# A fused attention and adapter-network block: logits, values and fills in pairs of steps, gate rows later, half an output projection earlier

## The chip, the cores and the metric

The kernel runs on one core of one Trainium2 chip. The metric is the device time of one launch in microseconds (us). The kernel before took 1315.23 us as the median of three runs, from 1310.58 to 1323.12.

## The reference

Everything is float32: a batch of 2 sequences of 2048 tokens with 256 features.

```python
mod = (silu(c) @ wmod).reshape(2, 6, 1, -1)          # sa, ca, ga, sb, cb, gb
ga, gb = bounded away from zero, at least 0.25 in size
h = layernorm(x) * (1 + ca) + sa
q, k, v = split(h @ W_qkv.T + b_qkv)                 # 16 heads of 16 features
o = softmax(causal(q k^T / 4)) v
x = x + ga * (o @ W_out.T + b_out)
h = layernorm(x) * (1 + cb) + sb
mole(x, W, b, A, B, R) = x W + b + 1/8 * sum_e softmax(x R)_e * (x A_e) B_e   # 3 experts, rank 8
return x + gb * mole(relu(mole(h, W1, ...)), W2, ...)    # 256 -> 1024 -> 256
```

## The kernel before, in words

The 4096 tokens are eight blocks of 512. To keep float32's precision, an operand of most products is split into a high part (rounded) and a low part (the rest), and a product is three passes, high x high, high x low, low x high (`product`, L391). The split's high part is mostly written by ScalarE (ACT), the low part by VectorE (DVE).

**First stage.** For each block DVE normalises x, TensorE (PE) transposes it (`turn`, L761), ACT scales and shifts it (`modulate`, L1024), DVE makes the low part (L1153), PE projects to queries and keys (`project_qk`, four chunks of six matmuls over 512 columns) and to values (`project_v`, 24 matmuls over 256 columns); ACT and DVE write high and low parts of queries and keys (L1031, L1165), which SyncE's queue (SP) stores to HBM and loads back as stacks of heads (L438, L453). Ahead of block 0's projections PE computes the modulation columns (L742) and the sixteen matmuls of the two gate rows (`gate_rows`, L751), which ACT copies out (L1046) before it goes on to block 1. GpSimd (POOL) clears rows of the stacks meanwhile (L585).

**Attention** runs over 32 units (4 heads of one sequence and 512 queries), in 320 steps of 128 keys. The logits stand transposed (keys on partitions), and the row maximum has to be known before a step: it is taken in advance from a second computation of the logits with queries on partitions. So PE has three kinds of work. `logits` (L875): four matmuls a step, one a head, on 64 rows of the array each, two heads at a time on the two halves, into three banks in turn. ACT takes the exponential of each (L1074) into `prob`. `values` (L893): eight matmuls of a step (four heads beside one another on 32 columns each, in two float32 passes), accumulated in one bank; they run two steps behind (`PV_LAG`). `fill` (L855): a tile of the maximum computation for a later unit, mostly four or two matmuls, that DVE reduces (L1222, L1218) out of two double banks. Diagonal tiles and steps get a mask added by small bf16 matmuls (L811). PE's order in a step: `values(n-2)`, logits of heads 0 and 1, up to two fills, logits of heads 2 and 3, more fills. Which fills stand in which step is a table (`ORDER`, made by `slots`); it holds 610 fills and isn't changed. A logit matmul waits until the exponential three before it is done (its bank), a fill until DVE has reduced the tile two before it.

**The network.** For each block i PE computes eight inner tiles (`hidden`, six matmuls over 512 columns and one low-rank matmul L954) in two banks; ACT empties each twice with relu (L1114: full, then high part) and DVE subtracts to the low part (`hid_low`, L1365). In between stand the low-rank tail of block i-1 and, after the fourth tile, the output projection of block i+1 (`project_out`, 24 matmuls). DVE then makes its residual, statistics and normalised rows, PE transposes them, and so on; `down` (L965) is the second layer, four groups of 24 matmuls, whose first one follows the high and low parts as they come. The projection's operand `oT` is split by ACT (`o_high`, L1084) and DVE (`low_o`, L1260) at the head of block i, after POOL has normalised the loaded rows (L694). POOL also adds residuals (L710, L699). Each engine works in the order written; waits are on semaphores.

## Time and profile before

| | |
|---|---|
| median of three runs | 1315.23 us |
| the profiled execution's own time | 1316.99 us |
| its span | 1315.0 us |
| PE busy | 1222.3 us (93%), 9456 matmuls |
| DVE busy | 934.4 us (71%) |
| ACT busy | 800.2 us (61%) |
| POOL busy | 183.3 us (14%) |
| mean clock granted to PE | 0.959 of full speed |

The profile is of one execution. Its times count from the span's start. A matmul's duration reaches from its start to a modelled end, and the next may stream earlier; what separates two of them is read from their starts. The idle time in brackets is that of the engine just before the instruction, with what ended it.

### The profile page before, as it was taken

To read this page: it belongs to the slowest core of one execution; us is meant where nothing else is said; L and a number is where in the kernel's file an instruction comes from. 1 tells how busy PE (TensorE), PEld (TensorE's weight loads), DVE (VectorE), ACT (ScalarE), POOL (GpSimd) and SP (SyncE) were. 2 spreads that over 40 slices of the span, in tenths; PEclk is the share of its full clock that TensorE was granted. 3 is DMA by queue.
4 is the path that set the end of the run, shared out by engine and by line. 5 is a ranking of instruction groups with operands and counts; after the bars stand their busy time and mean duration, and the time that the engine had idled before them with its cause. 6 is when DMAs were issued, how large, how long until landed. Compare 5 with 4: busy or idle time off the path is not lost.

```text
span 1315.0 us, 23664 instructions
## 1 busy us (share of the span) xinstructions
PE 1222.3 (93%) x9456; PEld 709.5 (54%) x9456; DVE 934.4 (71%) x1247; ACT 800.2 (61%) x1611; POOL 183.3 (14%) x153
## 2 busy tenths in 40 slices
PE   7988789999999999999999999999989999999997
PEld 6765333444444344444444444334334888888886
DVE  4877897888787888777888778776531477776653
ACT  4441466777667777767777767776664455454442
POOL 5205600000112000000000000201010133232310
PEclk9997799999999999999999989999787999999998
DMA  5793120031142022022022013400000122211100
GB/s 169 245 289 140 51 64 10 16 83 29 35 107 60 9 64 54 10 62 71 10 54 56 10 32 102 113 1 9 11 10 22 45 64 65 54 50 38 53 17 33
DMA packets 58118, 79.53 MB, mean 60 GB/s; under 512 B 12680, under 2 KB 28752, under 8 KB 58008
## 3 DMA queue, kind: packets, MB, share of 16 engines
q1 hardware_dynamic: 58008, 78.01, 20.3%
q8 instruction: 75, 1.23, 0.4%
q14 instruction: 35, 0.29, 0.1%
HBM read 47.57 MB, written 29.62 MB: 59 GB/s over the span
## 4 chain that ended last, share of the span: by engine, by line
PE 68%; DVE 17%; ACT 8%; issue 4%; SPq 2%; DMA 2%; ACTq 0%; DVEq 0%
PE ps L893 21%; PE ps L875 17%; PE ps L855 9%; PE ps L965 7%; PE ps L391 6%; ACT prob L1074 6%; PE ps L811 6%; DVE mx L1222 5%; DVE hid_lo L1365 4%; DVE xhat L419 1%; DVE stats L409 1%; SPq L453 1%; DMA xs<-in_x 1%; ACT o_sb L1059 1%; DVE x L1270 1%
## 5 line engine op out<-in xcount | busy, mean ns | idle before, releaser
L1074 ACT ACTIVATE prob<-ps 128x512 f32<-128x512 f32 (+3 forms) x1280 | 597.8, 536 | 267.9 <-PE ps L811 137.9
L1222 DVE TENSOR_REDUCE mx<-ps 128x2 f32<-128x1024 f32 (+1 forms) x512 | 591.5, 1187 | 164.1 <-PE ps L855 92.9
L875 PE MATMUL ps<-qst,kst 64*128 64x512 f32 (+3 forms) x1280 | 379.5, 450 | 14.9 <-ACT prob L1074 9.1
L875 PEld LDWEIGHTS ps<-qst,kst 64*128 64x128 f32 x1280 | 174.8, 188 | 325.9 <-ACT prob L1074 284.0
L893 PE MATMUL ps<-prob,vw 128*32 128x512 f32 (+3 forms) x2560 | 309.6, 557 | 9.2 <-ACT o_sb L1059 9.1
L855 PE MATMUL ps<-kst,qst 62*128 62x512 f32 (+3 forms) x1280 | 248.8, 419 | 23.3 <-DVE mx L1222 19.1
L855 PEld LDWEIGHTS ps<-kst,qst 62*128 62x128 f32 x1280 | 125.9, 193 | 68.6 <-DVE mx L1222 58.8
L811 PE MATMUL ps<-mask_kh,eye_h 64*128 64x128 bf16 x1024 | 100.8, 227 | 0.0
L893 PEld LDWEIGHTS ps<-prob,vw 128*32 128x32 f32 x2560 | 51.9, 109 | 74.9 <-ACT prob L1074 49.8
L1365 DVE TENSOR_TENSOR hid_lo<-hidf,hid_hi 128x512 fp32r<-128x512 f32 x64 | 73.1, 1182 | 13.8 <-ACT hid_hi L1114 13.7
L1218 DVE TENSOR_REDUCE mx<-ps 128x4 f32<-128x512 f32 x64 | 59.8, 954 | 21.1 <-PE ps L811 21.1
L965 PE MATMUL ps<-w_hi,hid_hi 128*128 128x284 f32 x256 | 71.9, 306 | 2.2 <-ACT hid_hi L1114 2.2
L1114 ACT ACTIVATE hidf<-ps,b_sb 128x512 f32<-128x512 f32 x64 | 43.9, 686 | 48.5 <-PE ps L954 48.5
L641 POOL COPY vw<-v_nat 128x1024 f32<-128x1024 f32 x8 | 8.3, 1039 | 466.1 <-PE ps L893 466.0
L965 PE MATMUL ps<-w_lo,hid_hi 128*128 128x284 f32 x256 | 70.2, 300 | 0.0
L811 PE MATMUL ps<-mask_qh,eye_h 64*128 64x128 bf16 x1024 | 66.1, 225 | 0.0
L391 PE MATMUL ps<-hT_hi,w_hi 128*128 128x512 f32 x128 | 53.6, 419 | 9.0 <-ACT hid_hi L1114 9.0
L1097 ACT ACTIVATE gexp<-gexp 128x12 f32<-128x12 f32 x16 | 3.4, 213 | 82.6 <-DVE gexp L1335 82.6
L811 PEld LDWEIGHTS ps<-mask_kh,eye_h 64*128 64x128 bf16 x1024 | 43.0, 97 | 17.3 <-issue 6.7
L965 PEld LDWEIGHTS ps<-w_hi,hid_hi 128*128 128x128 f32 x256 | 49.6, 194 | 4.1 <-ACT hid_hi L1114 3.8
L391 PE MATMUL ps<-hT_hi,w_lo 128*128 128x512 f32 x128 | 51.3, 401 | 0.0
L391 PE MATMUL ps<-hT_lo,w_hi 128*128 128x512 f32 x128 | 51.2, 400 | 0.0
(157 smaller groups left out, 1358.0 us busy)
## 6 DMA issues: line engine op xcount, KB each, us to landing
qk_parts<-parts SPq DMA_DIRECT2D x32, 512.0 KB, 4.9
qst<-qk_parts SPq DMA_DIRECT2D x192, 64.0 KB, 2.4
kst<-qk_parts SPq DMA_DIRECT2D x192, 64.0 KB, 2.4
xs<-in_x SPq DMA_DIRECT2D x16, 512.0 KB, 8.4
o_all<-o_sb SPq DMA_DIRECT2D x32, 256.0 KB
o_raw<-o_all SPq DMA_DIRECT2D x16, 256.0 KB
rd<-rden_rows SPq DMA_DIRECT2D x16, 256.0 KB
out<-y SPq DMA_DIRECT2D x8, 512.0 KB, 3.2
```

The lines of the kernel that those rows point to most:

```text
L391: last = pe.matmul(out, lhs(i, k), rhs(j, k), start=(start and k == 0 and n == 0), stop=(stop and k == chunks - 1 and n == len(PASSES) - 1))
L409: link(dve.bn_stats(stats[:, t, :], xs[:, t, :]), wait=(t == TT - 1))
L811: last = pe.matmul(ps[:, banks[par], col:col + P], eye_h[rows, half, :], table[rows, half, :], start=False, stop=True, skip_group_check=True)
L855: last = pe.matmul(ps[:, bank + par, at * width:(at + 1) * width], q[rows, p, J * BLK + r * P:J * BLK + (r + 1) * P], k[rows, p, cb * BLK: ...
L875: last = pe.matmul(ps[:, banks[par], 0:BLK - skip], kst[g % 2][rows, pair, t * P:(t + 1) * P], qst[g % 2][rows, pair, J * BLK + skip:(J + ...
L893: last = pe.matmul(ps[32 * h:32 * h + 32, O_BANK, skip:BLK], vw[:, g % 2, t, h, :], prob[:, n % P_BUFS, h, 0:BLK - skip], start=(t == 0), ...
L965: last = pe.matmul(ps[:, Y_BANK + t, 0:D + ZP], hid[u][:, m, t * P:(t + 1) * P], w2_p[v][:, m, :], start=(e == 0), stop=(e == len(order) - 1))
L1074: act.activation(prob[:, n % P_BUFS, h, 0:width], ps[:, L_BANK + i % L_BUFS, 0:width], ACT.Exp).then_inc(exp_done, 1)
L1114: act.activation(dst, ps[:, H_BANK + m % 2, :], ACT.Relu, bias=b1_sb[:, m:m + 1]).then_inc(f1_out, 1)
L1218: dve.tensor_reduce(mx[:, u % 2, :, :, r, cb], ps[:, bank:bank + 2, 0:2 * width].rearrange("p a (h x) -> p a h x", h=2), AX, ALU.max).then ...
L1222: dve.tensor_reduce(mx[:, u % 2, :, pairs[0], r, cb], ps[:, bank:bank + 2, 0:width], AX, ALU.max).then_inc(max_red, 1)
L1365: dve.tensor_tensor(hid[1][:, m, :], hidf[:, m % HRING, :], hid[0][:, m, :].bitcast(F32), ALU.subtract).then_inc(hid_lo_done, 1)
```

## The change

Three things are changed. In the first stage the gate rows come after block 0's projection to queries and keys, and ACT's copies of them after its work on block 0's chunks. In attention, two steps n and n+1 that are not diagonal, not the first two of a unit and have four fills or fewer together are issued in a new order, in which `values(n-2)` is cut in two halves of the columns and its parts and `values(n-1)` stand between logits; all other steps keep their order. In the network, the second half of the next block's output projection (tokens 256 to 511 of the block) comes ahead of the third inner tile, the first half stays after the fourth; `o_high` and `low_o` for that block move to the end of the block before.

```diff
@@ -789,12 +789,12 @@
                 pe.wait_ge(consts, 4)
                 turn(0)
                 columns(((2, 4), (3, 3)), COL_BANK - 1)
-                pe.wait_ge(setup, 2 * KC)
-                gate_rows()
                 pe.wait_ge(w_lo, 2)
                 project_qk(0, range(0, KC))
                 turn(1)
                 project_qk(0, range(KC, 2 * KC))
+                pe.wait_ge(setup, 2 * KC)
+                gate_rows()
                 project_v(0)
...
+                def output(bank, ts=range(TT)):
+                    for t in ts:
                         last = product(pe, ps[:, bank + t // 2, t % 2 * D:(t % 2 + 1) * D],
                                        lambda i, k: oT[i][:, k, t * P:(t + 1) * P],
                                        lambda i, k: wout_p[i][:, k, :], KC)
...
-                def logits(n, pair):
+                def logits(*heads):
+
+                    for n, h in heads:
+                        u, t = STEPS[n]
+                        g, J = UNITS[u]
+                        skip = skip_of(n)
+                        if n == FIRST[u] and h == 0:
+                            pe.wait_ge(m_in[u % 2], 16 * M_DMAS * (u // 2 + 1))
+                        until(pe, exp_done, 4 * n + h - L_BUFS + 1)
+                        rows = slice(h % 2 * STACK, h % 2 * STACK + ROWS + MROWS)
+                        last = pe.matmul(ps[:, L_BANK + (4 * n + h) % L_BUFS, 0:BLK - skip],
+                                         kst[g % 2][rows, h // 2, t * P:(t + 1) * P],
+                                         qst[g % 2][rows, h // 2, J * BLK + skip:(J + 1) * BLK],
+                                         start=True, stop=True)
+                        if not diagonal(n):
+                            last.then_inc(st_done, 1)
+                    if diagonal(heads[0][0]):
+                        mask_keys(heads)
...
+                    lo, hi = 0, BLK - skip
+                    if part == 0:
+                        hi = hi // 2
+                    if part == 1:
+                        lo = hi // 2
                     pe.wait_ge(exp_done, 4 * (n + 1))
...
                     for h in range(GH):
-                        last = pe.matmul(ps[32 * h:32 * h + 32, O_BANK, skip:BLK], vw[:, g % 2, t, h, :],
-                                         prob[:, n % P_BUFS, h, 0:BLK - skip],
-                                         start=(t == 0), stop=(n == LAST[u]), tile_position=(0, 32 * h))
-                    last.then_inc(pv_done, 1)
+                        last = pe.matmul(ps[32 * h:32 * h + 32, O_BANK, skip + lo:skip + hi], vw[:, g % 2, t, h, :],
+                                         prob[:, n % P_BUFS, h, lo:hi],
+                                         start=(t == 0 and part != 1), stop=(n == LAST[u] and part != 0),
+                                         tile_position=(0, 32 * h), skip_group_check=True)
+                    if part != 0:
+                        last.then_inc(pv_done, 1)
...
-                for n in range(NS):
-                    if n >= PV_LAG:
-                        values(n - PV_LAG)
-                    logits(n, 0)
-                    for e in ORDER[1 + n][:2]:
-                        fill(e)
-                    logits(n, 1)
-                    for e in ORDER[1 + n][2:]:
-                        fill(e)
-                for n in range(NS - PV_LAG, NS):
-                    values(n)
-
-
-                def project_out(i):
-                    pe.wait_ge(o_hi, i + 1)
-                    pe.wait_ge(o_lo, i + 1)
-                    until(pe, zg1_copied, i)
-                    until(pe, zg2_copied, i - 1)
-                    output(T_BANK).then_inc(p_done, 1)
+                for n in range(0, NS, 2):
+                    es = [*ORDER[1 + n], *ORDER[2 + n]]
+                    u = STEPS[n][0]
+                    if not diagonal(n) and n > FIRST[u] and len(es) <= 4:
+
+                        logits((n, 0), (n, 1))
+                        for e in es[0:1]:
+                            fill(e)
+                        logits((n, 2))
+                        values(n - 2, 0)
+                        logits((n, 3), (n + 1, 0))
+                        for e in es[1:2]:
+                            fill(e)
+                        values(n - 2, 1)
+                        logits((n + 1, 1))
+                        for e in es[2:3]:
+                            fill(e)
+                        logits((n + 1, 2), (n + 1, 3))
+                        values(n - 1)
+                        for e in es[3:]:
+                            fill(e)
+                    else:
+                        for m in (n, n + 1):
+                            if m >= PV_LAG:
+                                values(m - PV_LAG)
+                            logits((m, 0), (m, 1))
+                            for e in ORDER[1 + m][:2]:
+                                fill(e)
+                            logits((m, 2), (m, 3))
+                            for e in ORDER[1 + m][2:]:
+                                fill(e)
+                values(NS - 2)
+                values(NS - 1)
+
+
+                def project_out(i, half):
+
+
+                    if half == 1:
+                        pe.wait_ge(o_hi, i + 1)
+                        pe.wait_ge(o_lo, i + 1)
+                        until(pe, zg1_copied, i)
+                        output(T_BANK, range(TT // 2, TT))
+                    else:
+                        until(pe, zg2_copied, i - 1)
+                        output(T_BANK, range(TT // 2)).then_inc(p_done, 1)
...
@@ -984,6 +1027,8 @@
                     pe.wait_ge(zg1_copied, i + 1)
                     hidden_low_rank(i, 0)
                     hidden_low_rank(i, 1)
+                    if i + 1 < NBLK:
+                        project_out(i + 1, 1)
                     for m in range(2, FC):
                         hidden(i, m)
                         hidden_low_rank(i, m)
@@ -992,7 +1037,7 @@
                         if m == 3 and i >= 1:
                             down_low_rank(i - 1)
                         if m == 3 and i + 1 < NBLK:
-                            project_out(i + 1)
+                            project_out(i + 1, 0)
...
                 root(1)
-                act.wait_ge(rows_done, 1)
-                for v in range(2):
-                    act.copy(gates[:, v].rearrange("p b d -> p (b d)"), ps[:, V_BANK + v, :]).then_inc(rows_out, 1)
                 act.wait_ge(setup, 2 * KC + 1)
                 for n in range(NBLK):
                     if n + 1 < NBLK:
@@ -1051,6 +1093,11 @@
                     if n + 2 < NBLK:
                         root(n + 2)
                     high(n)
+                    if n == 0:
+                        act.wait_ge(rows_done, 1)
+                        for v in range(2):
+                            act.copy(gates[:, v].rearrange("p b d -> p (b d)"),
+                                     ps[:, V_BANK + v, :]).then_inc(rows_out, 1)
...
                 attention_over(act)
                 exponentials(0, z1_sub, z1_exp)
+                o_high(1)
                 for i in range(NBLK):
                     if i >= 1:
                         exponentials(i - 1, z2_sub, z2_exp)
-                    if i + 1 < NBLK:
-                        o_high(i + 1)
                     gated_in(i)
                     for m in range(FC):
                         hidden_out(i, m)
@@ -1131,6 +1177,8 @@
                     if i + 1 < NBLK:
                         modulate2(i + 1)
                         exponentials(i + 1, z1_sub, z1_exp)
+                    if i + 2 < NBLK:
+                        o_high(i + 2)
...
                 route_in(0)
+                low_o(1)
                 for i in range(NBLK):
                     front, back = i + 1 < NBLK, i >= 1
                     if back:
                         route_hidden(i - 1)
                         gate_y(i - 1)
-                    if front:
-                        low_o(i + 1)
                     for m in range(4):
                         hid_low(i, m)
                     if back:
@@ -1408,6 +1455,8 @@
                     if front:
                         low2(i + 1)
                         route_in(i + 1)
+                    if i + 2 < NBLK:
+                        low_o(i + 2)
```

`mask` is replaced by `mask_queries` and `mask_keys`, which issue the same matmuls for a list of heads.

Engine PE in attention, two steps with two fills each, before. The names are `qst` and `kst` for the stacks of queries and keys, `prob` for exponentials and `vw` for values; L875 are logits, L855 fills, L893 values:

```order
L893 MATMUL ps<-prob,vw 32x512 x4
L875 MATMUL ps<-qst_107,kst_106 128x512 x2
L855 MATMUL ps<-kst_106,qst_107 128x512 x4
L875 MATMUL ps<-qst_107,kst_106 128x512 x2
L893 MATMUL ps<-prob,vw 32x512 x4
L875 MATMUL ps<-qst_107,kst_106 128x512 x2
L855 MATMUL ps<-kst_106,qst_107 128x512 x4
L875 MATMUL ps<-qst_107,kst_106 128x512 x2
```

The same engine for a new pair of steps (L882 are logits, L863 fills, L907 values):

```order
L882 MATMUL ps<-qst_76,kst_75 128x512 x2
L863 MATMUL ps<-kst_106,qst_107 128x512 x2
L882 MATMUL ps<-qst_76,kst_75 128x512
L907 MATMUL ps<-prob,vw 32x256 x4
L882 MATMUL ps<-qst_76,kst_75 128x512 x2
L863 MATMUL ps<-kst_106,qst_107 128x512 x2
L907 MATMUL ps<-prob,vw 32x256 x4
L882 MATMUL ps<-qst_76,kst_75 128x512
L863 MATMUL ps<-kst_106,qst_107 128x512 x2
L882 MATMUL ps<-qst_76,kst_75 128x512 x2
L907 MATMUL ps<-prob,vw 32x512 x4
L863 MATMUL ps<-kst_106,qst_107 128x512 x2
```

One group of values is now two groups over 256 columns, with three logits and a fill between them; the other group over 512 columns stands at the end, ahead of the fourth fill.

Engine DVE at the end of a block of the network and the head of the next, before (`gmax` to `zg` is the routing, `y<-ps,gates` the gated output):

```order
L1349 TENSOR_TENSOR zg<-zf,zg 128x4x24
L1334 TENSOR_REDUCE gmax<-ps 128x4
L1335 TENSOR_TENSOR gexp<-ps,gmax 128x12
L1338 TENSOR_REDUCE gsum<-gexp 128x4
L1339 RECIPROCAL gsum<-gsum 128x4
L1340 SCALAR_TENSOR_TENSOR gexp<-gexp,gsum 128x12
L1343 TENSOR_TENSOR zf<-ps,gexp 128x96
L1348 CAST zg<-zf 128x4x24 x2
L1349 TENSOR_TENSOR zg<-zf,zg 128x4x24
L1372 TENSOR_TENSOR y<-ps,gates 128x1024
L1260 TENSOR_TENSOR oT_lo<-o_raw,oT_hi 128x1024
L1365 TENSOR_TENSOR hid_lo<-hidf,hid_hi 128x512 x4
```

And now:

```order
L1397 TENSOR_TENSOR zg<-zf,zg 128x4x24
L1308 TENSOR_TENSOR oT_lo<-o_raw,oT_hi 128x1024
L1382 TENSOR_REDUCE gmax<-ps 128x4
L1383 TENSOR_TENSOR gexp<-ps,gmax 128x12
L1386 TENSOR_REDUCE gsum<-gexp 128x4
L1387 RECIPROCAL gsum<-gsum 128x4
L1388 SCALAR_TENSOR_TENSOR gexp<-gexp,gsum 128x12
L1391 TENSOR_TENSOR zf<-ps,gexp 128x96
L1396 CAST zg<-zf 128x4x24 x2
L1397 TENSOR_TENSOR zg<-zf,zg 128x4x24
L1420 TENSOR_TENSOR y<-ps,gates 128x1024
L1413 TENSOR_TENSOR hid_lo<-hidf,hid_hi 128x512 x4
```

The operand's low part has moved from between the gated output and the first low parts of the inner tiles to between the two routings.

## Rows read from the trace of the kernel before

**Rows 1.** Busy time by stretch: us, then each engine, granted clock, DMA share, GB/s.

```profile
112.00:1011.00 899.00, 847.19 (x7228) 378.31 (x7230) 673.92 (x728) 613.72 (x1315) 80.28 (x77) 0.96 0.16 42
1011.00:1315.00 304.00, 281.83 (x1740) 250.18 (x1732) 186.86 (x353) 137.08 (x217) 75.25 (x28) 0.95 0.16 47
```

**Rows 2.** Who waited for whom: us in total, times, longest us.

```profile
PEld ps L875 <- ACT prob L1074: 284.0, 446, 2.7
...
ACT prob L1074 <- PE ps L875: 128.3, 179, 2.7
```

**Rows 3.** Timeline of one attention step: start, us, engine, instruction, [idle before].

```profile
643.02 0.50 PE L875 MATMUL ps<-qst,kst 64*128 64x512 f32 x2
643.13 0.19 PEld L855 LDWEIGHTS ps<-kst,qst 62*128 62x128 f32 x2
643.36 0.69 PE L855 MATMUL ps<-kst,qst 62*128 62x512 f32 x4
...
643.62 2.06 ACT L1074 ACTIVATE prob<-ps 128x512 f32<-128x512 f32 x4 [0.60 <-PE ps L875]
...
644.26 0.18 PEld L875 LDWEIGHTS ps<-qst,kst 64*128 64x128 f32 x1 [0.42 <-ACT prob L1074]
...
644.69 1.06 PE L893 MATMUL ps<-prob,vw 128*32 128x512 f32 x8
...
645.69 0.50 PE L875 MATMUL ps<-qst,kst 64*128 64x512 f32 x2
...
646.28 2.07 ACT L1074 ACTIVATE prob<-ps 128x512 f32<-128x512 f32 x4 [0.60 <-PE ps L875]
```

**Rows 4.** Timeline: values over 256 columns and what follows; the masks of a fill.

```profile
177.38 0.64 PE L893 MATMUL ps<-prob,vw 128*32 128x256 f32 x8
177.95 0.50 PE L875 MATMUL ps<-qst,kst 64*128 64x512 f32 x2
...
654.22 0.40 PE L811 MATMUL ps<-mask_qh,eye_h 64*128 64x128 bf16 x8
```

**Rows 5.** Timeline of the first stage.

```profile
17.40 6.16 PE L751 MATMUL ps<-wmod_sb,silu_wide 128*128 128x256 f32 x16
...
23.60 1.07 ACT L1046 COPY gates<-ps 128x512 f32<-128x512 f32 x2 [6.78 <-PE ps L751]
...
30.10 3.67 DVE L419 TENSOR_SCALAR xhat<-xs,mv,rstd 128x256 f32<-128x256 f32 x4
...
37.46 1.21 DVE L1171 TENSOR_TENSOR v_nat<-ps,bv_sb 128x1024 f32<-128x1024 f32 x1
...
46.03 2.88 SPq L438 DMA_DIRECT2D qk_parts<-parts  x4
49.02 5.01 SPq L453 DMA_DIRECT2D qst<-qk_parts  x6
```

**Rows 6.** Timeline of one block of the network.

```profile
1094.37 1.22 DVE L1260 TENSOR_TENSOR oT_lo<-o_raw,oT_hi 128x1024 fp32r<-128x1024 f32 x1
...
1094.53 3.30 POOL L710 TENSOR_TENSOR y<-y,x1b 128x1024 f32<-128x1024 f32 x1 [12.66 <-DVE y L1372]
...
1095.81 6.59 DVE L1365 TENSOR_TENSOR hid_lo<-hidf,hid_hi 128x512 fp32r<-128x512 f32 x4 [0.23 <-ACT hid_hi L1114]
...
1095.83 0.50 PE L391 MATMUL ps<-hT_hi,w_hi 128*128 128x512 f32 x1 [1.12 <-ACT hid_hi L1114]
...
1113.59 0.40 PE L965 MATMUL ps<-w_hi,hid_lo 128*128 128x284 f32 x1 [0.21 <-DVE hid_lo L1365]
```

**Rows 7.** Two neighbouring matmuls of the 24 of one output projection.

```profile
1100.12 0.28 PE L391 MATMUL ps<-wout_hi,oT_hi 128*128 128x256 f32 x1
...
1100.24 0.28 PE L391 MATMUL ps<-wout_lo,oT_hi 128*128 128x256 f32 x1
```

**Rows 8.** Busy time by stretch: two blocks of the network, columns as in rows 1.

```profile
1132.00:1168.00 36.00, 34.41 (x222) 30.58 (x222) 25.87 (x47) 17.98 (x29) 11.02 (x5) 1.00 0.23 59
1168.00:1205.00 37.00, 35.44 (x220) 31.70 (x218) 24.27 (x46) 17.32 (x29) 10.11 (x5) 0.95 0.20 58
```

More of the change, by code:

```diff
@@ L803, in _, with mask_queries @@
                     project_v(n)
-                def mask(banks, col, table):
+                def mask_queries(bank, col):
                     for half in range(2):
@@ L860, in fill, with values @@
                         for at in range(len(pairs)):
-                            last = mask((bank, bank + 1), (at + 1) * width - P, mask_qh)
+                            last = mask_queries(bank, (at + 1) * width - P)
                     last.then_inc(fill_done, 1)
-                def logits(n, pair):
+                def logits(*heads):
+                    for n, h in heads:
+                        u, t = STEPS[n]
[13 more added lines that the diff above has]
+                        mask_keys(heads)
+                def values(n, part=None):
                     u, t = STEPS[n]
@@ L868, in logits @@
                     skip = skip_of(n)
[L869 to L887 removed]
+                    lo, hi = 0, BLK - skip
[3 more added lines that the diff above has]
+                        lo = hi // 2
                     pe.wait_ge(exp_done, 4 * (n + 1))
[L889 removed]
+                    if n == FIRST[u] and part != 1:
                         pe.wait_ge(v_wide, g + 1)
```

34 lines of the change are left out of this document (9 added, 25 removed).

## The prediction

> **What bounds the kernel now.** I first read the stages side by side [rows 1]: after the projections of queries, keys and values (to 112 us) come attention (899 us, two thirds of the span), and then output projection and the two-layer network (304 us). TensorE counts as busy for 94 and 93% of these two, but a matmul's record runs past the moment at which the next one may stream, so this doesn't say TensorE is full. In attention VectorE is busy 674 of 899 us and ScalarE 614, so neither of these is full either. The waits [rows 2] say what couples them: logit weight loads wait 284 us in 446 places for an exponential, and exponentials wait 128 us for logits. It is a ring, not one full engine.
>
> The ring shows in the timeline of one steady step [rows 3]. Call the four logits of a step L0 to L3, their exponentials E0 to E3, the group of eight value matmuls V, the row-maximum tiles F0 and F1. E0 starts at 643.62; three logit banks mean that L3 may only go when E0 is done, and its load stands at 644.26 (0.64 later). V follows at 644.69 (0.43), the next L0 at 645.69 (1.00), the next E0 at 646.28 (0.59). 0.64 + 0.43 + 1.00 + 0.59 = 2.66 us a step, 5.33 for two; meanwhile ScalarE works 2.06 and idles 0.60. The fills hang beside this ring. The projection stage and the network have rings of their own, below.
>
> **The change, part by part.** My sum is against the profiled execution, 1317.0 us (span 1315.0 and about 2 around it); the median of the runs is 1315.2, 1.8 lower, and the runs lie 12.5 apart.
>
> *Gate rows later (first stage).* The sixteen gate-row matmuls take 6.16 us ahead of the first query/key projection [rows 5]; ScalarE stands 6.78 us for them, behind them its modulation of block 1. Nothing there needs the gates. Moved behind that projection, they leave TensorE at 17.5 to twelve projection matmuls (512 columns, 0.23 each: 2.8 us) and eight transposes (about 0.8), so ScalarE can start at about 21.5, some 5 us sooner than now (gate copies to 24.7, then as many matmuls and transposes). VectorE can't use all of it: its rescaling (at 30.10) is slowed to 3.67 us while GpSimd clears rows. Project_v(0) now waits for the gate copies: gate rows end near 30.3, copies (two in 1.07) near 31.4, project_v(0), 24 matmuls at 0.119 [rows 7], near 34.3. VectorE's v_rows then starts at 34.3 instead of 37.5, and its order carries 2.6 to 3.1 us on to the second store of parts, at 46.03. From there SP issues stores and stack loads one behind the other (six loads in 5.01 us from 49.02), so it and DMA do the same work from an earlier start. I take -2.6 us. Ends: 0 (SP and DMA don't move), -5 (the whole shift of ScalarE).
>
> *Two-step order (attention).* The table of fills makes 59 of the 160 pairs of steps take the new branch, in 25 chains: 13 of one pair, 7 of three, 5 of five. No work goes; V of step n-2 is cut into two halves. A half is a group of 256 columns, which the diagonal steps show: 0.57 us from its start to the next logit, against 1.00 [rows 4]. So two halves cost +0.14, and one more change into and out of V adds 0.09 (0.43 from L3's load to V, against 0.34 from L0's to the fill that follows at once) and 0.11 for a load of weights that can't run ahead; a stream of 512 columns alone is 0.34 - 0.11 = 0.23. I walked one full pair with the distances of rows 3: an exponential starts 0.49 after its logit's stream (0.60 less the load) or 0.48 after the one before (2.06 for four), is done 0.60 later, and lets a load go 0.05 after; V starts 0.09 after the last stream. Counted from L0's stream: F0 0.23, L2 0.46, half V 0.78, L3's load 1.35. L4 needs E1, done at 0.49 + 0.48 + 0.60 = 1.57, so it loads at 1.62, not 1.35; then F1 1.96, half V 2.28, L5's load 2.85, F2 3.19, L6 and L7 3.42, whole V 3.74, F3's load 4.73, next L0 at 5.07. Without the wait for E1 TensorE would need 4.80. The ring of rows 3 is gone, yet **TensorE itself** now sets 5.07, for 5.33 before: -0.26 a pair. At a chain's start the missing V lets E0 follow the last exponential at once (-0.74). At its end the price comes back: V(n-1), F3 and then the ordinary V(n) stand in a row before the next L0, and ScalarE runs dry for 1.9 us (the last pair +0.94 over an ordinary one, a single pair +1.00). A longer chain's first pair has ScalarE still busy and gains 0.19. So a chain of one gives -0.74 + 1.00 = +0.26, of three -0.74 - 0.19 - 0.26 + 0.94 = -0.25, of five -0.77: 3.4 - 1.8 - 3.9 = -2.3 us. In 33 of the 59 pairs fills are diagonal tiles with masks behind them (eight mask matmuls 0.40 [rows 4]). Before, TensorE's wait of 0.42 a step [rows 3] hid them; now nothing does. I take 0.15 a pair, +5. Part: +2.6. Ends: all pairs at 4.80 would make it -13; pairs no quicker than 5.33 with masks in full (0.4 x 33) about +16.
>
> VectorE is no bound: four fills at 1.14 are 4.6 us of 5.07, and each finds its bank free in the walk.
>
> *Half projection ahead of the third inner tile (network).* TensorE idles 1.12 us before the third tile of every block, for ScalarE to empty its bank [rows 6]. Twelve of the 24 projection matmuls, 0.119 each [rows 7], 1.43 us, go in there: the third tile starts about 0.05 later and the fifth 1.3 earlier. What is late next? The last product with the low part waits at 1113.59 for VectorE [rows 6], whose row of work is unbroken before it; the residual's statistics in it also hold ScalarE's sixth eviction. So most of 1.3 becomes a wait there. What does shorten VectorE's row is the split of the operand that leaves it (1094.37, 1.22 us): GpSimd's addition began at 1094.53 and took 3.30, of which it stood about 1.0 for the split to end (1095.59). The four low parts behind took 6.59 us, 1.65 each, the first two held while GpSimd adds. With GpSimd done 0.8 earlier, the fourth low part is then bound by ScalarE's eviction, 0.45 earlier than now. The split itself goes into VectorE's idle time at the block's end, between two routings, and delays the second by an estimated 0.15, under cover of TensorE's next tiles. ScalarE's cast goes there too, into its idle time; its input, GpSimd's normalised block, has been ready for some us by then. -0.45 in six blocks: -2.7. Ends: 7 x -1.3 = -9 if VectorE isn't the bound; +1 if it is and the routing delay counts.
>
> Sum: -2.6 + 2.6 - 2.7 = -2.7, so 1314.3 for a profiled execution, **1313** against the median.
>
> **Rivals.** *The two-step order pays in full.* If L4 doesn't in effect wait for E1, pairs come at 4.80: 59 x -0.27 = -16 on top of the sum, so **1297**. For it: of 5.33, ScalarE needs 4.1 and VectorE 4.6. Against: E1's end follows from L1's start in every step of rows 3.
>
> *Slower: the changes of tile shape and the ends of chains eat the gain.* V is a group of 128-row, 32-column tiles, logits and fills use 64 rows. Place: the two halves and the V, F3, V at a chain's end. With each half 0.1 dearer and masks in full: 118 x 0.1 + 8 = +20 on top, **1333**; it is over 1% slower from 0.13 a half on. For it: 25 chain ends, 13 after a single pair. Against: the 256-column group is a direct row [rows 4]. The Trainium skill, "TensorEngine Tiling (Array Packing)", Key Properties, says that a change of tiling mode drains the engine; the 0.09 above is what the trace shows of it, and were the drain as long as a stream (0.23 instead of 0.09, both ways), the 59 added groups would give some 59 x 0.28 = +17 us and a time of 1330.
>
> *The clock.* A network block takes 36 us at the full clock of 2.4 GHz; the next, with a stretch at 1.2 GHz in it (mean granted clock 0.95), takes 37 and more [rows 8], some 1.5 us longer. Three of the eight have one. Were TensorE's longer wait for VectorE followed by such a stretch in every block, five more would cost 5 x 1.5 = 8 us: **1321**, inside the forecast's case.
>
> **Chances.** A measurement of this kernel can't tell less than about 1% (13 us) from no change. Forecast with the clock's case 0.62, its own range 1303 to 1324; in full 0.26; slower 0.12. To hold 8 in 10 I take **1299 to 1324**. Faster by over 1% 0.26, within 0.62, slower 0.12.
>
> **What would show it.** In the changed trace a run of full pairs in attention should come every 5.07 us (5.33 is the old ring, 4.80 the rival), with the load of a logit waiting 0.27 for ScalarE behind L3; after a chain's last pair ScalarE should idle 1.9 us once. The third inner tile should show no idle time before it, and the last low part's product should wait 1 us or more. The second store of parts should be issued about 2.6 earlier, and attention begin so much earlier. I am wrong if the attention stage moves by over 10 us, or if the network's block drops from 35.9 to under 35.

## The result, and the profile after

| | before | changed |
|---|---|---|
| median of 20 runs each, us | 1315.05 | 1306.32 |
| lowest to highest, us | 1307.02 to 1328.27 | 1301.44 to 1316.13 |
| ratio, 95% interval | | 0.9935 (0.9915 to 0.9956) |
| span of the profiled execution, us | 1315.0 | 1302.4 |
| mean granted clock | 0.959 | 0.965 |

The changed kernel is 8.5 us faster (5.8 to 11.2, from the ratio), under 1% but beyond the scatter. The forecast was -2.7. Granted clock is the share of TensorE's full 2.4 GHz that the chip let it have; "half clock" below is time at 1.2 GHz.

I cut both spans at the same five points: the first exponential, those of steps 80, 160 and 280, and the last one. First the busy time by stretch of the kernel before, then of the changed one (us, then busy time of PE, its weight loads, DVE, ACT and POOL, granted clock, DMA share, GB/s).

```profile
130.10:365.00 234.90, 217.81 (x1903) 97.89 (x1901) 194.48 (x208) 152.58 (x329) 32.07 (x29) 0.97 0.15 40
365.00:574.30 209.30, 202.80 (x1810) 91.88 (x1809) 167.72 (x179) 152.13 (x329) 13.22 (x22) 1.00 0.18 49
574.30:889.90 315.60, 303.77 (x2619) 134.85 (x2616) 248.15 (x259) 228.34 (x493) 11.24 (x7) 0.99 0.20 52
889.90:1010.20 120.30, 108.74 (x813) 46.50 (x813) 47.57 (x64) 79.08 (x166) 8.11 (x4) 0.87 0.03 11
1010.20:1315.00 304.80, 282.63 (x1744) 250.47 (x1741) 186.86 (x353) 137.40 (x219) 75.25 (x28) 0.95 0.16 47
```

```profile
128.10:365.30 237.20, 220.44 (x1991) 101.93 (x1988) 195.24 (x208) 152.79 (x328) 32.06 (x29) 0.95 0.15 40
365.30:577.30 212.00, 205.49 (x1928) 96.55 (x1928) 168.57 (x179) 152.11 (x328) 13.23 (x22) 0.99 0.18 49
577.30:892.00 314.70, 304.26 (x2811) 141.38 (x2810) 249.38 (x259) 228.15 (x493) 11.24 (x7) 0.99 0.19 53
892.00:1003.50 111.50, 102.90 (x885) 47.81 (x885) 47.60 (x64) 79.30 (x166) 8.11 (x4) 0.92 0.03 12
1003.50:1302.40 298.90, 278.74 (x1744) 248.14 (x1736) 180.77 (x353) 137.49 (x219) 69.84 (x28) 0.96 0.16 48
```

Of the 12.6 us between these two executions the start gives 2.0, the attention up to step 280 costs 4.1 (+2.3, +2.7, -0.9), its last forty steps give 8.8 and the network 5.9. But the granted clock differs too: 0.87 against 0.92 in the last forty steps. So one pair of profiles can't price an edit; the experiments below give more executions of each order.

**Attention.** A full inner pair of steps (compare [rows 3]), from the timeline of the changed kernel:

```profile
226.25 2.56 ACT L1121 ACTIVATE prob<-ps 128x512 f32<-128x512 f32 x5 [0.61 <-PE ps L882]
226.56 0.64 PE L907 MATMUL ps<-prob,vw 128*32 128x256 f32 x8
...
227.12 0.18 PEld L882 LDWEIGHTS ps<-qst,kst 64*128 64x128 f32 x1 [0.41 <-ACT prob L1121]
...
227.39 0.18 PEld L882 LDWEIGHTS ps<-qst,kst 64*128 64x128 f32 x1
...
228.06 0.64 PE L907 MATMUL ps<-prob,vw 128*32 128x256 f32 x8
...
229.51 1.06 PE L907 MATMUL ps<-prob,vw 128*32 128x512 f32 x8
...
230.84 0.40 PE L882 MATMUL ps<-qst,kst 64*128 64x512 f32 x2
...
231.33 1.08 ACT L1121 ACTIVATE prob<-ps 128x512 f32<-128x512 f32 x2 [0.60 <-PE ps L882]
```

From exponential to exponential it is 231.33 - 226.25 = 5.08. The prediction's walk put the half group at 0.78; with 226.56 taken as that point, L3 stands at 1.34, L4 at 1.61, the second half at 2.28, the whole group at 3.73 and the next L0 at 5.06: each within 0.01 or 0.02 of the walk, the wait of L4 too (227.39 - 227.12 = 0.27). At the end of this chain:

```profile
246.42 0.50 PE L863 MATMUL ps<-kst,qst 62*128 62x512 f32 x2
246.85 1.07 PE L907 MATMUL ps<-prob,vw 128*32 128x512 f32 x8
247.85 0.49 PE L882 MATMUL ps<-qst,kst 64*128 64x512 f32 x2
...
248.56 1.09 ACT L1121 ACTIVATE prob<-ps 128x512 f32<-128x512 f32 x2 [1.92 <-PE ps L820]
```

Fill, ordinary value group and logits stand in a row, and ScalarE idles 1.92.

Two pairs before the end of the same chain stands a pair whose fills are diagonal tiles. It reaches from 236.44 to 242.03, 5.59 us. Mask matmuls (L811) stand between its other work, the last of them right before the next logits:

```profile
238.12 0.44 PE L811 MATMUL ps<-mask_qh,eye_h 64*128 64x128 bf16 x8
...
241.36 0.29 PE L811 MATMUL ps<-mask_qh,eye_h 64*128 64x128 bf16 x4
241.46 0.48 PE L882 MATMUL ps<-qst,kst 64*128 64x512 f32 x2
...
242.03 2.19 ACT L1121 ACTIVATE prob<-ps 128x512 f32<-128x512 f32 x4 [0.86 <-PE ps L882]
```

All such pairs are like this. In the changed kernel's trace the five inner pairs with four full fills take 5.08 to 5.10, and ten inner pairs with diagonal tiles among their four fills (12 to 22 mask matmuls in a pair) take 5.52 to 5.63, more than the old order's 5.33. (One more, in the last forty steps, takes 5.47; it stands behind a long fill, below.)

The waits of the whole kernel (compare [rows 2]):

```profile
PEld ps L882 <- ACT prob L1121: 211.3, 408, 2.7
ACT prob L1121 <- PE ps L820: 161.3, 247, 8.8
...
ACT prob L1121 <- PE ps L882: 96.6, 148, 2.3
```

Logit loads wait 73 us less and exponentials 32 us less for logits, 23 more for masks (137.9 before), and the time of the stage hardly moved. Less waiting inside the chains is paid at their ends and in the pairs with masks.

**First stage.** TensorE's rows, changed kernel (compare [rows 5]):

```profile
18.60 0.63 PE L391 MATMUL ps<-hT_lo,wqkv_hi 128*128 128x512 f32 x1
19.02 0.63 PE L391 MATMUL ps<-hT_hi,wqkv_lo 128*128 128x512 f32 x1
...
24.64 0.40 PE L391 MATMUL ps<-hT_lo,wqkv_hi 128*128 128x512 f32 x1
24.88 0.39 PE L391 MATMUL ps<-hT_hi,wqkv_lo 128*128 128x512 f32 x1
...
27.20 3.62 PE L751 MATMUL ps<-wmod_sb,silu_wide 128*128 128x256 f32 x16
```

And those of the other engines and the queue:

```profile
24.22 0.78 ACT L1069 ACTIVATE hf<-ps,mod 128x512 f32<-128x512 f32 x1 [7.41 <-PE ps L761]
...
27.44 4.30 DVE L419 TENSOR_SCALAR xhat<-xs,mv,rstd 128x256 f32<-128x256 f32 x4
...
35.43 1.21 DVE L1219 TENSOR_TENSOR v_nat<-ps,bv_sb 128x1024 f32<-128x1024 f32 x1
...
38.95 4.00 DVE L419 TENSOR_SCALAR xhat<-xs,mv,rstd 128x256 f32<-128x256 f32 x4
...
45.44 2.87 SPq L438 DMA_DIRECT2D qk_parts<-parts  x4
```

The projection's matmuls stand 0.42 apart, where the prediction had 0.23, and the gate rows now take 3.62 instead of 6.16. TensorE ran at the slower pace up to about 23 us in both kernels: the move exchanged which work pays for it. The pace is that of the same matmuls at 79 us,

```profile
79.58 0.63 PE L391 MATMUL ps<-hT_lo,wqkv_hi 128*128 128x512 f32 x1
80.01 0.63 PE L391 MATMUL ps<-hT_hi,wqkv_lo 128*128 128x512 f32 x1
```

whose granted clock is 0.50 by the busy time of that stretch:

```profile
78.50:85.00 6.50, 5.98 (x14) 4.75 (x15) 3.48 (x5) 2.62 (x4) 0.00 (x0) 0.50 0.86 185
```

**Network.** One block of the changed kernel (compare [rows 6]):

```profile
1079.68 1.22 DVE L1308 TENSOR_TENSOR oT_lo<-o_raw,oT_hi 128x1024 fp32r<-128x1024 f32 x1
...
1085.74 2.40 POOL L710 TENSOR_TENSOR y<-y,x1b 128x1024 f32<-128x1024 f32 x1 [14.06 <-DVE y L1420]
...
1087.02 5.08 DVE L1413 TENSOR_TENSOR hid_lo<-hidf,hid_hi 128x512 fp32r<-128x512 f32 x3 [1.36 <-ACT hid_hi L1161]
...
1102.38 0.40 PE L1008 MATMUL ps<-w_hi,hid_hi 128*128 128x284 f32 x1 [0.63 <-ACT hid_hi L1161]
...
1104.22 0.40 PE L1008 MATMUL ps<-w_hi,hid_lo 128*128 128x284 f32 x1 [0.20 <-DVE hid_lo L1413]
```

GpSimd's addition takes 2.40 instead of 3.30, and the 1.12 of idle time ahead of the third tile is gone. In its place TensorE waits 0.22 (at 1101.22) and 0.63 in the second layer for ScalarE's evictions. VectorE's first low part starts 1.28 us behind the start of the addition in both kernels (1095.81 and 1094.53 before, 1087.02 and 1085.74 now), held by ScalarE's high part in both; so it isn't the split's absence from VectorE's row that lets the low parts start sooner. The fourth ends 7.87 us behind the addition's start before and 7.30 now: the 0.57 lies in the low parts beside the addition.

### The profile page after: what moved, and what is told of

It is laid out like the page before. It is cut to its first block, busy times and chain, and to the rows that moved or that the text cites. A ratio compares the mean times of both kernels' runs of the same rounds, so it can differ in the third digit from the quotient of the medians.

```text
span 1302.4 us, 24602 instructions
## 1 busy us (share of the span) xinstructions
PE 1218.0 (94%) x9928; PEld 723.5 (56%) x9928; DVE 933.2 (72%) x1247; ACT 800.5 (61%) x1611; POOL 178.0 (14%) x153
## 3 DMA queue, kind: packets, MB, share of 16 engines
q8 instruction: 78, 1.28, 0.4%
## 4 chain that ended last, share of the span: by engine, by line
PE 67%; DVE 12%; ACT 9%; issue 8%; SPq 2%; DMA 1%; POOL 0%; POOLq 0%; ACTq 0%; DVEq 0%
PE ps L907 21%; PE ps L882 17%; PE ps L863 9%; PE ps L391 8%; ACT prob L1121 7%; PE ps L1008 5%; DVE mx L1270 5%; PE ps L820 4%; PE ps L811 2%; DVE xhat L419 1%; DVE hid_lo L1413 1%; SPq L453 1%; ACT o_sb L1106 1%; DVE stats L409 1%; DMA wqkv_sb<-in_wqkvT 1%
## 5 line engine op out<-in xcount | busy, mean ns | idle before, releaser
L882 PE MATMUL ps<-qst,kst 64*128 64x512 f32 (+3 forms) x1280 | 387.0, 446 | 18.9 <-ACT prob L1121 14.3
L882 PEld LDWEIGHTS ps<-qst,kst 64*128 64x128 f32 x1280 | 183.9, 188 | 270.2 <-ACT prob L1121 211.3
L907 PE MATMUL ps<-prob,vw 128*32 128x512 f32 (+3 forms) x3032 | 317.8, 492 | 3.4 <-ACT o_sb L1106 3.4
L863 PE MATMUL ps<-kst,qst 62*128 62x512 f32 (+3 forms) x1280 | 288.7, 425 | 21.5 <-DVE mx L1270 18.1
L863 PEld LDWEIGHTS ps<-kst,qst 62*128 62x128 f32 x1280 | 137.1, 193 | 95.4 <-DVE mx L1270 51.5
L907 PEld LDWEIGHTS ps<-prob,vw 128*32 128x32 f32 x3032 | 60.5, 108 | 86.9 <-issue 38.7
L1413 DVE TENSOR_TENSOR hid_lo<-hidf,hid_hi 128x512 fp32r<-128x512 f32 x64 | 68.0, 1095 | 20.7 <-ACT hid_hi L1161 20.6
L811 PE MATMUL ps<-mask_qh,eye_h 64*128 64x128 bf16 x1024 | 74.4, 225 | 0.0
L820 PEld LDWEIGHTS ps<-mask_kh,eye_h 64*128 64x128 bf16 x1024 | 42.6, 97 | 17.1 <-issue 5.8
L1008 PEld LDWEIGHTS ps<-w_lo,hid_hi 128*128 128x128 f32 x256 | 51.3, 200 | 0.4
```

The lines of the kernel that those rows point to most:

```text
L811: last = pe.matmul(ps[:, bank + par, col:col + P], eye_h[rows, half, :], mask_qh[rows, half, :], start=False, stop=True, skip_group_check= ...
L820: last = pe.matmul(ps[:, L_BANK + (4 * n + h) % L_BUFS, 0:P], eye_h[rows, half, :], mask_kh[rows, half, :], start=False, stop=True, skip_g ...
L863: last = pe.matmul(ps[:, bank + par, at * width:(at + 1) * width], q[rows, p, J * BLK + r * P:J * BLK + (r + 1) * P], k[rows, p, cb * BLK: ...
L882: last = pe.matmul(ps[:, L_BANK + (4 * n + h) % L_BUFS, 0:BLK - skip], kst[g % 2][rows, h // 2, t * P:(t + 1) * P], qst[g % 2][rows, h // ...
L907: last = pe.matmul(ps[32 * h:32 * h + 32, O_BANK, skip + lo:skip + hi], vw[:, g % 2, t, h, :], prob[:, n % P_BUFS, h, lo:hi], start=(t == ...
L1008: last = pe.matmul(ps[:, Y_BANK + t, 0:D + ZP], hid[u][:, m, t * P:(t + 1) * P], w2_p[v][:, m, :], start=(e == 0), stop=(e == len(order) - 1))
```

## The experiments

All are made from the same two kernels. A ratio is to the kernel before on the same chip.

**Each part alone, and the change without the two-step order.** `gate_only`, `two_step_only` and `half_only` are the kernel before with one part; `no_two_step` is the changed kernel with one line edited:

```diff
-                    if not diagonal(n) and n > FIRST[u] and len(es) <= 4:
+                    if False:
```

> The kernel before with one part of the change: the gate rows and their copies later, attention and network as before. My theory (the shift of the first stage reaches attention as it is): attention starts 1.4 us (as read between the two traces) to 2.6 us (my prediction) earlier and nothing else moves, 1313 to 1314 us, ratio 0.998 to 0.999. Rival (stretches at the lower clock in the first stage take as much back): attention starts within 0.5 us of before.

> The kernel before with the two-step order alone. My theory, now: on the even ground of steps 0 to 279 the new order costs 3 to 5 us net (pairs of 5.08 between, +0.9 to 1.0 at each chain's end); what the profile of the change shows after step 280, 8.8 us less, is clock (half-clock stretches of 17 us there instead of 44) and comes with the two-step order if the order's denser work at the end of attention is its cause. Then 1308 to 1312 us, and half-clock time after step 280 under 25 us. Rival (the clock at the end of attention is chance, the same kernel shows either): ratio 1.002 to 1.004 and half-clock stretches of 40 us or so there.

> The kernel before with the network's part alone: half of the output projection ahead of the third inner tile, the operand's split one block sooner. My theory: a block goes from 35.9 to 35.35 us, as in the profile of the change, six times, so -3.3 us, ratio 0.997. Rival (the gain in the network, 6.5 us between the two traces, is the third tile's idle time and not the low parts): -6 us or more, ratio 0.995.

> The changed kernel without its two-step order: gate rows later and half the projection earlier. If the two-step order is a net loss (its walk says +2.6 to +4 us) and the end-of-attention clock is chance, this is 4 us faster than the changed kernel, near 1303, ratio to before 0.990. If the two-step order brings the better clock at the end of attention, this is slower than the changed kernel, 1310 us, ratio 0.996.

| kernel | median, us | ratio | 95% interval | by the prediction's terms, us | measured, us |
|---|---|---|---|---|---|
| gate rows later | 1312.96 | 0.9974 | 0.9946 to 1.0002 | -2.6 | -3.4 |
| two-step order | 1314.99 | 0.9989 | 0.9961 to 1.0017 | +2.6 | -1.4 |
| half projection and split | 1312.52 | 0.9962 | 0.9933 to 0.9991 | -2.7 | -5.0 |
| without the two-step order | 1308.25 | 0.9943 | 0.9914 to 0.9972 | -5.3 | -7.5 |

The three parts add to -9.8, the whole gives -8.5: nothing links them. The two-step order is worth nothing that a measurement can tell, by itself (0.9989) or on top of the rest (0.9935 against 0.9943), so the expectation that leaving it out would gain about 4 us isn't borne out. Nor did either expectation of `two_step_only` hold: its half clock after step 280 fell to 3.4 us in the profile, well under the 25 of the theory, but the ratio is neither the theory's (1308 to 1312 us) nor the rival's (1.002 to 1.004). In the profile of `gate_only` attention starts at 129.4, 0.8 us sooner than in the kernel before and not the 1.4 to 2.6 of the expectation; `half_only`'s blocks take the 35.3 that was expected.

**The same runs at one clock.** Every run lists its mean granted clock, and the scatter follows it. A line fitted through 132 runs (of the kernel before, the changed one, the four above and `two_step_tail` below), with one slope for all, falls by 0.93 us for each 0.001 of mean clock and leaves a scatter of 1.4 us. (0.001 of 1315 us is 2.6 us of half clock, so this is 0.35 us for each us of it.) Read off that line at a mean clock of 0.960, against the kernel before (whose runs on the two chips lie 0.3 us apart there):

| kernel | at clock 0.960, us | 95% |
|---|---|---|
| gate rows later | -1.1 | 0.9 either way |
| two-step order | -0.9 | 0.9 |
| half projection and split | -4.3 | 0.9 |
| without the two-step order | -5.2 | 0.9 |
| two-step order in the last forty steps only (below) | -8.8 | 0.9 |
| the change | -6.8 | 0.8 |

The parts add to -6.3 for -6.8. These are estimates from that line, and they are tighter than the ratios, since most of the scatter is clock.

**Where the order's cost and gain lie.** `two_step_tail` keeps it for the last forty steps only:

```diff
-                    if not diagonal(n) and n > FIRST[u] and len(es) <= 4:
+                    if n >= 280 and not diagonal(n) and n > FIRST[u] and len(es) <= 4:
```

> The changed kernel with its two-step order from step 280 on only. If the order loses on even ground (2.7 us in steps 80 to 159, read from the traces of e2 and e3) and gains only at attention's end, this is 3 to 5 us faster than the changed kernel: 1302, ratio 0.990. If its gain is not at the end, the ratio is that of e4, 0.994.

Measured: 1307.38, ratio 0.9947 (0.9926 to 0.9968), that of `no_two_step` and not the 0.990 that a gain at attention's end would have given. But at one clock it lies 3.7 us (2.6 to 4.8) below `no_two_step` and 2.1 us (1.1 to 3.1) below the changed kernel: the order gains some 3.7 in the last forty steps and costs some 2 before them. The first profiles had shown 8.8 there, since most of it was clock. Each trace gives the time of a stretch and how much of it was granted half clock, both in us:

| kernel | order in the last forty steps | steps 80 to 159: time (half clock) | step 280 to the end: time (half clock) |
|---|---|---|---|
| before | old | 209.3 (0) | 120.4 (32.1) |
| no_two_step | old | 209.2 (0) | 120.4 (32.1) |
| gate_only | old | 209.2 (0) | 115.2 (18.8) |
| half_only | old | 209.3 (0) | 112.6 (10.2) |
| split_move (below) | old | 210.7 (3.4) | 112.5 (10.2) |
| two_step_tail | two-step | 209.3 (0) | 113.1 (22.0) |
| changed | two-step | 212.0 (3.4) | 111.5 (17.1) |
| two_step_only | two-step | 212.0 (3.4) | 107.3 (3.4) |
| halves_alone (below) | old | 209.3 (0) | 115.2 (19.0) |

The busy time by stretch of `gate_only` and of `two_step_only` shows the two ends of the last column (the mean clock stands third from the right):

```profile
889.00:1004.20 115.20, 103.43 (x813) 45.27 (x813) 47.58 (x64) 78.99 (x166) 8.11 (x4) 0.92 0.03 11
```

```profile
893.20:1000.50 107.30, 98.22 (x885) 45.72 (x885) 47.49 (x64) 79.00 (x167) 8.12 (x4) 0.98 0.04 12
```

With the old order the last stretch grows by (120.4 - 112.6) / (32.1 - 10.2) = 0.36 us for each us at half clock. On that line 17.1 us of it would give 115.1, and the changed kernel has 111.5. So of the 8.8 that the two profiles gave there, 5.2 are clock and some 3.6 the order. A piece at full clock in both agrees: steps 280 to 291 take 34.1 us with the two-step order and 35.9 with the old one, in the traces of before, `no_two_step`, `two_step_tail` and changed alike. In steps 80 to 159 it costs 212.0 - 210.7 = 1.3 at equal clock; in steps 160 to 279, 314.8 at 3.4 us of half clock against 313.4 at the same 3.4 (`two_step_tail`, old order there), 1.4, or 0.7 against the middle of the other old-order executions (312.4 at none, 315.9 at 6.8); in steps 0 to 79 nothing that the scatter of seven old-order executions lets show. Together -0.9 to -1.6, where the fitted line gives -0.9 by itself and -1.6 on top of the other two parts. So traces and timings agree on both signs: a loss of about 2 before step 280 and a gain of about 3.6 behind it.

Where the gain lies can be read in steps 280 to 291, at full clock in both orders. By pairs from step 280, `two_step_only` against before, they change by -0.88 (the entry), -0.17, -0.56 (one fill), +0.02 (one fill, an output projection of 24 matmuls), -1.16 (the pair behind it) and +0.94 (the end): -1.8. That the pair behind the projection gains most no walk had, and why it does was not tried.

**The split's move, and the halves.** `split_move` has the operand's split at the end of the block before and the projection in one piece; `halves_alone` has the halves and leaves the split at the block's head.

```diff
                         if m == 3 and i + 1 < NBLK:
-                            project_out(i + 1)
+                            project_out(i + 1, 1)
+                            project_out(i + 1, 0)
```

> The kernel before with one piece of the network's part: the operand's split at the end of the block before, the projection in one piece after the fourth tile. My theory (GpSimd's addition no longer stands behind the split, and VectorE's row is the bound): a block takes 35.4 to 35.5 us, the same as with both pieces, and TensorE still idles 1.12 us before the third tile. Rival (the halves fill idle time that counts): the block stays at 35.9.

> The kernel before with the output projection cut in two halves, one ahead of the third inner tile, and the operand's split left at the head of the block where it was. Theory (the split's move gives the block its whole 0.55, the halves nothing of their own in steady blocks): blocks without a stretch at half clock take 35.9 as before, or more, since the half projection in front of the third tile now also waits for the low part of the operand that VectorE writes only at the head of the block. Rival (each piece gives a part): 35.5 or less. The time itself, one run: 1313 to 1317.

Each was run once: 1312.22 and 1315.81 us, which alone can't be told from the kernel before; the traces can. A network block without a stretch at half clock, from first relu to first relu: 35.9 before, 35.34 changed, 35.32 with the split's move alone, 36.5 with the halves alone. So the move of the split (VectorE's part and ScalarE's together) gives the whole gain of a steady block, and the halves alone lose 0.6. `split_move` keeps the idle time before the third tile and has GpSimd's short addition:

```profile
1093.61 2.37 POOL L710 TENSOR_TENSOR y<-y,x1b 128x1024 f32<-128x1024 f32 x1 [13.95 <-DVE y L1417]
...
1094.92 0.50 PE L391 MATMUL ps<-hT_hi,w_hi 128*128 128x512 f32 x1 [1.12 <-ACT hid_hi L1158]
```

In `halves_alone` the half projection stands for the low part that VectorE has only begun, and the addition is long again:

```profile
1089.07 1.22 DVE L1305 TENSOR_TENSOR oT_lo<-o_raw,oT_hi 128x1024 fp32r<-128x1024 f32 x1
...
1089.23 3.30 POOL L710 TENSOR_TENSOR y<-y,x1b 128x1024 f32<-128x1024 f32 x1 [12.68 <-DVE y L1417]
1090.38 0.36 PE L391 MATMUL ps<-wout_hi,oT_hi 128*128 128x256 f32 x1 [0.96 <-issue]
```

Only the first block gains from the halves: 34.71 changed, 34.70 with the halves alone, 35.62 before.

**Another order for the same pairs.** The chain's ends cost what its middle gains. In `v_ahead` a fill and a half value group come before the second logit, so that the ring's wait for a bank falls under them:

```diff
-                        logits((n, 0), (n, 1))
+                        logits((n, 0))
                         for e in es[0:1]:
                             fill(e)
-                        logits((n, 2))
                         values(n - 2, 0)
-                        logits((n, 3), (n + 1, 0))
+                        logits((n, 1), (n, 2))
                         for e in es[1:2]:
                             fill(e)
                         values(n - 2, 1)
-                        logits((n + 1, 1))
+                        logits((n, 3), (n + 1, 0))
                         for e in es[2:3]:
                             fill(e)
-                        logits((n + 1, 2), (n + 1, 3))
+                        logits((n + 1, 1))
                         values(n - 1)
+                        logits((n + 1, 2), (n + 1, 3))
                         for e in es[3:]:
                             fill(e)
```

`v_ahead_first` also takes first pairs of a unit and pairs with five fills, 93 instead of 59: `if not diagonal(n) and n >= 2 and len(es) <= 5`.

> The changed kernel with another order in the same 59 pairs: L0, F0, half V, L1, L2, F1, half V, L3, L4, F2, L5, whole V, L6, L7, F3, so that two logits and a fill stand between the last V and the next pair. My theory (what the two-step order loses is the wait of L4 for E1 and the row V, F3, V at a chain's end): a pair inside a chain falls from 5.08 to about 4.85 us, a chain's last pair no longer takes 0.9 more than before, and attention loses about 15 us against the changed kernel, so 1291 us, ratio to before 0.982. Rival (halves of V cost by themselves, whatever the order): no faster than the changed kernel, ratio 0.993.

> As e5, and the order is also used for the first pair of a unit and for pairs with five fills. By the same walk chains are longer and fewer: another 7 us off, 1284 to 1286 us, ratio 0.977. Rival (the copy of a finished unit's output stalls ScalarE in the first pair when V of the old unit stands late): no better than e5.

Measured: `v_ahead` 1290.52, ratio 0.9826 (0.9805 to 0.9848); `v_ahead_first` 1283.35, ratio 0.9765 (0.9749 to 0.9781), both about as expected, and faster than both kernels (five runs each). The chain of five pairs from step 106, from exponential to exponential: an inner pair 4.94 (changed 5.09, before 5.33), the two with masks 5.19 and 5.46 (changed 5.63 and 5.53), the last pair 5.94 (changed 6.39). Two logits now stand between `values(n-1)` and the last fill, so ScalarE has work while TensorE does the ordinary group behind the chain. The edit changes middle and end of a chain at once, and the two weren't tried apart. An inner pair of `v_ahead_first`:

```profile
227.14 0.64 PE L907 MATMUL ps<-prob,vw 128*32 128x256 f32 x8
227.71 0.51 PE L882 MATMUL ps<-qst,kst 64*128 64x512 f32 x2
228.25 1.58 ACT L1121 ACTIVATE prob<-ps 128x512 f32<-128x512 f32 x3 [0.27 <-PE ps L882]
...
228.61 1.07 PE L907 MATMUL ps<-prob,vw 128*32 128x512 f32 x8
229.61 0.50 PE L882 MATMUL ps<-qst,kst 64*128 64x512 f32 x2
...
230.14 1.58 ACT L1121 ACTIVATE prob<-ps 128x512 f32<-128x512 f32 x3 [0.32 <-PE ps L882]
```

ScalarE's idle times in the pair are 0.27 and 0.32, against 0.35 and 0.60 in the changed kernel. Steps 80 to 159 take 206.3 with `v_ahead` and 204.0 with `v_ahead_first`, both at full clock, against 209.3.

## Why the prediction held, step by step

The forecast (1313, within 1%) held in kind: no part pays over 1%, and 1306.32 lies in the range. It was 6 us off in size. At one clock the three terms came out at -1.1, -0.9 and -4.3 for -2.6, +2.6 and -2.7, and some 2 us of the 8.5 are clock. So the sum is near the result partly because its errors go both ways: that is luck, and the wide range covered it.

- **Gate rows: the sum too high, the way to it wrong.** ScalarE was to start at about 21.5 and started at 24.22, since twelve projection matmuls took 5.3 instead of 2.8 [rows 5]. VectorE's rescaling of block 1 started 2.66 sooner (27.44 for 30.10) and `v_nat` 2.03. But the rescaling took 4.30 for 3.67; it lies wholly under GpSimd's clearing of rows (27.54 to 35.67) in both traces, and what made it longer is open. That of block 2 took 4.00 for 2.57: starting at 38.95 instead of 40.98, it now lies 3.85 instead of 1.8 beside GpSimd's splits of weights, which end near 42.8 in both. The second store of parts left 0.59 sooner, not the 2.6 predicted. Attention's first exponential came 2.0 sooner in this pair of traces (128.1 for 130.1); over the others it lies at 128.6 to 131.1 with the gate rows later and 129.2 to 130.7 without. What the timing gives (-3.4, from -7.1 to +0.3) can't be told from nothing, at one clock it is -1.1 (0.2 to 2.0 less), and the step "its order carries 2.6 to 3.1 us on to the second store" failed. The Trainium skill, "SBUF — State Buffer", Who interferes with whom, says that VectorE's `tensor_scalar` in its two-port mode and GpSimd lock each other out of a shared port pair; this rescaling, 1.38 by itself and 4.30 beside the clearing, agrees.
- **Two-step order: the walk right, its sum 3.5 us too high, and the miss lies in the last forty steps.** Inner pair without masks 5.08 to 5.10 (5.07 predicted), first pair of a longer chain 5.15 (-0.18 for -0.19), ScalarE idle once for 1.92 (1.9). A chain's end costs 6.39 for 5.47, +0.92 (+0.94). The term for masks, 0.15 a pair, is mis-sized: inner pairs with masks take 0.4 to 0.55 more than those without. A chain of five with its entry, two of its pairs with masks, took 32.2 for 32.1 where the prediction's terms give -0.5; a single pair with four diagonal fills took 11.77 for 11.04 with its entry (+0.4 predicted), three without masks 10.9 for 10.8 (+0.3), and two with one diagonal fill 11.5 for 11.6 (+0.4). By luck such errors cancel before step 280: the terms give +2.4 there and the runs about +2. What the sum missed is the last forty steps, +0.3 by its terms and some -3.6 by the runs. The walk took every pair as one with four fills, and five of the nine there have one or two (a pair with one fill took 4.79 for 5.34, with two 4.75 for 5.34); and the pair behind the output projection gained 1.16. The rival "pays in full" (4.80 a pair) is refuted by the pair and by L4's wait of 0.27; so is the drain of 0.23 a change, by which a pair would have taken 5.07 + 0.28 = 5.35. The Trainium skill, "TensorEngine Tiling (Array Packing)", Key Properties, says that a change of tiling mode drains the engine and names no length; the pairs without masks, within 0.03 of a walk with 0.09 for it, agree with a short one.
- **Network: the mechanism right, the size 1.6 us low, and one sign missing.** GpSimd's addition got 0.90 shorter (0.8 predicted), the block 0.55 (0.45), and `split_move` shows that the split's move alone does it. The step "the last low part's product should wait 1 us or more" failed: it waits 0.20. The wait went to ScalarE's evictions instead (0.22 and 0.63). Only the first block has a wait of 1.14 for the low part; there the halves gain 0.9, which the prediction didn't count. 0.9 and 0.55 in each of six blocks are 4.2 us, and the runs at one clock give 4.3. Of the network's 5.9 in the traces the seven block periods give 3.0 (less than 4.2, since one more of them has a stretch at half clock, 1.5), 2.2 stand before the first block, where the kernel before ran at half clock for 12.3 us and this one for 3.4, and 0.7 behind them.
- **Clock: priced right.** A block with a stretch at half clock takes 36.88 for 35.34, +1.5. The changed kernel's profile has four among the seven periods, the one before three.

In the "slower" rival the place was right for the masks and wrong for the halves: its masks in full (0.4 a pair) came true in the inner pairs, its 0.1 a half did not. Its bound of 0.13 a half for a loss of over 1% goes with the small mask term; with masks in full, 8 us more, it would be 0.07.

What is clock in the -8.5 us is an estimate: -6.8 at one clock leaves some 1.7. Why an execution meets much or little half clock stays open. At attention's end one order had 10.2 us of it in one execution and 32.1 in another, worth 7.8 us, and nothing that I ran steers it.

## What to carry to other kernels

When work is moved from one place of a ring to another, walk the entry and the exit of the rearranged stretch as well as its middle, and each kind of member: here a plain pair in the middle gained 0.26, one with masks lost 0.2 to 0.3, since the old order's wait had hidden the masks, and the exit cost 0.92. The order that left the fast consumer something to do at the exit, and shorter waits in the middle, paid (1.7% in the same 59 pairs, 2.4% in 93). When a wait disappears, ask which piece did it: the split's move, which takes a VectorE operation off a GpSimd one, gave the whole 0.55 a steady block, and filling 1.12 us of TensorE's idle time gave something in the first block only. Compare two profiles only where their granted clock is the same; and where many runs list their clock, compare the kernels at one clock, which showed here 3.7 us that the medians hid.

## What the runs showed of the hardware

- TensorE worked at the half pace up to about 23 us from the span's start (512 columns in 0.42, and 0.23 to 0.24 behind it) although the column of the granted clock says 1.00 there: the trace's clock records begin at 23.8 (22.4 in the kernel before). Early rows of this kernel must be priced by their own spacing.
- The same order met 10.2 to 32.1 us of half clock at attention's end in different executions, with TensorE busy 89 and 90% of the stretch. A us of it cost 0.36 there, 1.5 / 3.4 = 0.45 in a network block, and 0.35 over whole runs (0.93 us for each 0.001 of mean clock).
- A GpSimd addition with both inputs in SBUF took 2.40 where no such operation of VectorE ran at its start, and 3.30 where it started 0.16 behind VectorE's subtraction with two SBUF inputs. It held VectorE as well: three low parts beside GpSimd's additions took 5.08, one by itself 0.69.
